# Edge network: transposed destination one-hots by a compare of two tensors

## The reference

```python
def _L1_gnn_ref(x, edge_index, edge_feat, W1, b1, W2, b2, W3, b3):
    source = edge_index[0]
    target = edge_index[1]
    edge = jnp.concatenate([x[source], x[target], edge_feat], axis=-1)   # 48 + 48 + 16
    h = jax.nn.relu(edge @ W1 + b1)                                      # hidden 128
    h = jax.nn.relu(h @ W2 + b2)
    message = h @ W3 + b3
    msum = jax.ops.segment_sum(message, target, num_segments=n)
    cnt = jax.ops.segment_sum(ones, target, num_segments=n)
    return x + msum / jnp.maximum(cnt, 1.0)[:, None]
```

## Time and profile before

| what | us |
|---|---|
| median of 3 runs | 8639.95 (8632.92 to 8644.36) |
| profiled execution, its span | 8640.6 |
| edge network: first gather to last gather | 5516.3 to 7547.1 |
| POOL busy with gathers (1568) | 1554.2 |
| DVE busy with L1849 (392) | 266.8 |
| PE waiting at L1930 for a gather | 263.4 |

### The profile page before, as it was taken

How to read it: one execution, slowest core, us unless ns; L and a number is a source line. 1 busy time by engine, 2 the same in 40 slices (tenths; PEclk the granted TensorE clock), 3 DMA queues, 4 the chain that set the end, 5 groups by cost and what they waited for, 6 DMA issues and landing times. The chain is left out here.

```text
span 8640.6 us, 563982 instructions
## 1 busy us (share of the span) xinstructions
PE 7490.3 (87%) x228719; PEld 6386.0 (74%) x228719; DVE 6536.9 (76%) x13039; ACT 4071.0 (47%) x9117; POOL 5548.3 (64%) x5894
## 2 busy tenths in 40 slices
PE   4967758889999999999999999499999899949794
PEld 4856648889999999999999999344444454449794
DVE  5779979978888898888888888544444444478787
ACT  1229969944444444444444444244444444424242
POOL 2520000068888888888888888477777777738384
PEclk7559975589999999999999999799999999979797
DMA  5210026689999999999999999433333333249495
GB/s 80 92 47 0 0 69 246 247 299 342 338 338 339 340 340 336 340 340 338 340 340 338 339 338 339 122 77 79 78 79 79 79 79 77 64 161 339 161 338 166
DMA packets 833483, 1832.18 MB, mean 212 GB/s; under 512 B 245310, under 2 KB 306774, under 8 KB 831838
## 3 DMA queue, kind: packets, MB, share of 16 engines
q1 hardware_dynamic: 752974, 1777.08, 58.4%
q0 software_dynamic: 59776, 46.03, 4.8%
q10 hardware_dynamic: 20624, 7.81, 0.5%
HBM read 1667.67 MB, written 157.79 MB: 211 GB/s over the span
## 5 line engine op out<-in xcount | busy, mean ns | idle before, releaser
L1491 PE MATMUL banks<-arena 128*128 128x48 bf16 x58800 | 2352.6, 184 | 5.4 <-issue 5.4
L1491 PEld LDWEIGHTS banks<-arena 128*128 128x128 fp8e4 x58800 | 2270.5, 95 | 5.9 <-issue 5.7
L1457 DVE TENSOR_TENSOR banks<-banks,wslot 128x384 f32<-128x384 f32 (+1 forms) x3600 | 1984.5, 569 | 343.8 <-PE banks L1491 309.8
L1391 POOL TENSOR_TENSOR arena<-arena 128x768 bf16<-128x768 f32 (+2 forms) x1200 | 1838.3, 1540 | 422.6 <-DVE arena L1461 414.1
L1323 ACT CAST arena<-banks 128x384 bf16<-128x384 f32 (+1 forms) x2400 | 1178.8, 493 | 1872.6 <-DVE banks L1457 1693.7
L1491 PE MATMUL banks<-xc,arena 128*128 128x48 bf16 x24500 | 1943.0, 184 | 62.0 <-DVEq L1470 14.9
L1491 PEld LDWEIGHTS banks<-xc,arena 128*128 128x128 fp8e4 x24500 | 1864.4, 95 | 164.5 <-issue 104.7
L1773 POOL DMA_INDIRECT f<-node_table,idx x1568 | 1554.2, 991 | 557.6 <-issue 466.9
L1461 DVE TENSOR_TENSOR arena<-banks,arena 128x384 f32<-128x384 f32 (+1 forms) x2400 | 1350.4, 574 | 95.4 <-ACT arena L1323 2.3
L1505 PE MATMUL banks<-arena 32*128 32x144 bf16 x80400 | 1374.8, 222 | 21.5 <-issue 13.3
L1505 PEld LDWEIGHTS banks<-arena 32*128 32x128 bf16 x80400 | 1261.2, 93 | 49.2 <-issue 17.8
(11 more groups left out here) (385 smaller groups left out, 13650.6 us busy)
## 6 DMA issues: line engine op xcount, KB each, us to landing
arena<-onehots SPq DMA_DIRECT2D x1200, 512.0 KB, 4.9
arena<-onehots SPq DMA_DIRECT2D x1500, 256.0 KB, 5.2
arena<-onehots SPq DMA_DIRECT2D x300, 576.0 KB, 5.8
arena<-onehots SPq DMA_DIRECT2D x300, 544.0 KB, 5.3
arena<-in_dst SPq DMA_DIRECT2D x195, 512.0 KB
arena<-onehots SPq DMA_DIRECT2D x300, 288.0 KB
onehots<-arena SPq DMA_DIRECT2D x100, 768.0 KB, 3.2
arena<-key_rows SPq DMA_DIRECT2D x196, 196.0 KB
```

Of the source, the lines that this page charges most:

```text
L1391: nc.gpsimd.tensor_tensor(mp_low[b], mp_rest[b], mp_mid[b], ALU.subtract).then_inc(lo_done[b], 1)
L1457: nc.vector.tensor_tensor(bank, bank, w, ALU.mult).then_inc(m_done, 1)
L1491: m = nc.tensor.matmul(to, g_ring[b][:, i * P:(i + 1) * P], x_part, start=c == 0, stop=c == 2)
```

## The change

The compare of `turn_dst` becomes another form of instruction. Before, VectorE compared one tensor with a scalar per partition, the column g of `row_w`. Now it compares two tensors: the second is the same column, read with a step of zero over all 4 x 128 elements. Place, order, destination, waits and signals stay as they are.

```diff
@@ -1846,8 +1846,8 @@
                         when(dve, dst_in[u], t * 16 + 16)
                         when(dve, transposed, q + (FREE - 1))
                         mine = dst_rows[:, u, :].rearrange("p (e k) -> p k e", k=TILES)[:, HALF * j:HALF * j + HALF, :]
-                        nc.vector.tensor_scalar(hotT[:, j, :].rearrange("p (k e) -> p k e", k=HALF), mine,
-                                                row_w[:, bass.ds(g, 1)], None, ALU.is_equal).then_inc(hotT_ready, 1)
+                        nc.vector.tensor_tensor(hotT[:, j, :].rearrange("p (k e) -> p k e", k=HALF), mine,
+                                                row_w[:, bass.ds(g, 1)].unsqueeze(2).broadcast_to([P, HALF, P]), ALU.is_equal).then_inc(hotT_ready, 1)
```

## The result

The changed kernel takes **8672.5 us** (median of 5 runs, 8669.4 to 8684.2); beside it the kernel before took 8641.1 (5 runs). The ratio is 1.0036, with an interval of 1.0024 to 1.0048: slower by about 31 us. The forecast was 8692, slower, with a range of 8622 to 8755. The profiled execution is 30.0 us longer than the one before.

The account below looks back on a forecast made before the run. GpSimd's gathers were taken to pace the edge stage. 8640.6 + 51 (gathers held longer) + 0 (VectorE's extra work, hidden) = 8692 us; the 8-in-10 range was 8622 to 8755.

Parts of the forecast that it names:

- What bounds the stage: Edge network's stage: GpSimd's gathers pace it one after the other, 1.25 us each, about 10 us a group.
- (a) the instruction's time: L1849: two-tensor form takes 1.07 us instead of 681 ns, priced from L947; ends 678 and 1225 ns.
- (b) VectorE's extra work at nothing: VectorE: 392 x 0.39 = 153 us more work, hidden off the path, put at 0.
- the nearest reader: L1939, taken to load one-hots that end behind L1849, with 0.49 us of room.
- (c) the gathers: Gathers stretched longer by L1849: +86 us for an even spread, +51 us after leaving out tied groups.
- evenly spread: Compares fall at any phase of the gathers' beat; each costs (T - 0.12)^2 / (2 x 1.25) on average.
- late moment: Late point of a gather held by the scalar L1849: 6 of 70 us of stretching, gone after the change.
- The share of tied groups: 80 of 196 groups, where TensorE waits for the gather, counted at no change; 0.59 of 86 us left.
- The 0.12 us: Taken off what is left of a running compare to get what a gather's start loses.
- the two-tensor form holds nothing: Rival: two-tensor L1849 does not hold gathers, all 55 us of its stretching go, 8586 us; 8%.
- The short compare: Rival: L1849 stays at 678 ns, only the late 6 us go, 8635 us; 8%.
- The engines falling into step: Rival: compares settle at a good phase of the gathers' beat, 15 us less than now, 8626 us; 14%.

Follow-up runs that it names:

- dense: Changed kernel's two-tensor compare reading 512 neighbouring row numbers instead of every eighth one: 8606.4 us, ratio 0.9963 to the kernel before.
- the one-tensor compare: Kernel before, its scalar compare given an unused running sum and the low 16 bits of row numbers as input: 8573.8 us, ratio 0.9924.
- the moved order: Changed kernel with the odd half-steps' compare L1849 placed behind the subtraction L1880: 8758.1 us, ratio 1.0133 to the kernel before.

## Why the prediction was right, and where its sizes were off

*What bounds the stage* was right: the table above is the same statement with eleven kernels.

*(a) the instruction's time*: 1.07 forecast, 1.076 measured. L947 was the right neighbour, and the stepping is the reason: dense, it takes 0.685.

*(b) VectorE's extra work at nothing*: right, and shown by the one-tensor compare, which is longer still. But I misread the nearest reader. The one-hots of L1862 that end at 7530.89 are not those that L1939 loads at 7531.38: they are made two half-steps ahead (`L_HOT` 8, `L_SUM` 10), so the room is a whole group's step, not 0.49 us. The reader with little room is L1930, whose weight load waits for L1849. What ended TensorE's idle time at L1930 (us, times), before and after:

```profile
  DVE arena L1849: 119.5, 150
```

```profile
  DVE arena L1849: 112.0, 106
```

So that did not grow either.

*(c) the gathers* is where the size was off: +51 forecast, +30 measured. By its own terms:

| term | forecast | measured |
|---|---|---|
| L1849 at the start, before | 49 | 40.2 |
| L1849 at the start, after | 141.5 evenly spread | 92.0 |
| late moment, freed | 6 | 12.1 |
| L1880 | no change | 10.1 less |

The growth at the start, scaled by 0.59 as I did, is 92.5 x 0.59 = 55, and 51.8 came. The miss is in the other two: the late moment was worth double, and L1880, which I left out of the sum, lost most of what it cost. I had found the 6 by taking two evenly spread terms from the 70, so all that the even spread said too much at the start was missing there; counting the late stretches in the trace of before would have given 12.

*The share of tied groups* came out near the mark, but its reason is half right. With a wait of over 0.3 us at L1930 as the sign of a tied group, there are 79 before and 103 after. They cost 0.54 us of stretching each before and 0.52 after: no change, as I had counted them, though they are not the same groups in the two traces. In the others it rose from 0.235 to 0.49, that is by 0.26 and not by the 0.44 of the even spread, so a phase decides there too. That 55 lies so near to 51.8 is therefore in part luck. And it is not a property of tied groups: in the moved order they cost 0.98 each. I can't say why the phases settle as they do in each kernel; the pairs' distance explains why one of two is paid, and a full account of where a pair begins against the beat stays open.

*The 0.12 us* at the end of a compare is 0.175 under the stepping two-tensor form. With it the even spread gives (1.076 - 0.175) squared / 2.5 x 392 = 127 instead of 141.5.

*The rivals.* That the two-tensor form holds nothing is refuted by 176 of 179 gathers. The Trainium skill, "SBUF — State Buffer", section "Who interferes with whom", has the rule that fits: a VectorE instruction with two inputs in SBUF contends with a GpSimd instruction that reads SBUF. The same section of the Trainium skill reports a probe in which `tensor_tensor` did not stall transfers. For these gathers the runs show otherwise: from 0.94 to 1.67 in the rows above. The short compare is refuted by 1076. The engines falling into step was half true: in 151 of 195 pairs one compare of the two comes out free, and the cost is 92 where the even spread has 127, though not below that of the kernel before.

## What to carry to other kernels

Where GpSimd's gathers pace a stage, sum their busy time first and compare kernels by it; then ask of each vector instruction not only how long it is but whether it reads one tensor or two, whether it works in the two-at-a-time form, and how its distance to the next such instruction stands to the gathers' beat. In these runs a long instruction that holds nothing was better than a short one that does (8574 against 8637), and two short ones were better than one long (8606 against 8673). An even spread of phases bounds such a cost well enough for its sign, but not for its size: the same edit cost 31 us in one order of the code and 101 in another.

## What was not expected of the hardware

A compare with a scalar that also writes a running sum takes 1134 ns and 83 for reading the sum, where the same without it takes 681, and it holds no gather at either moment. A vector instruction that reads one tensor from PSUM and one from SBUF (L1871) holds none either: in the trace after, 113 gathers started with more than 0.25 us of it left, and none was stretched. With the holds gone, TensorE waits for a gather in nearly every group, 193 times, but for a shorter time each (311 us, against 263 in 80 waits before; 97 of either is the first wait, ahead of the loop). Of waits over 2.2 us there are 3 instead of 34. Its granted clock, a mean over the span at 1.2 and at 2.4 GHz, was 0.906 to 0.938 of the higher level in the five runs, and 0.891 to 0.925 in the nine of the kernel before beside them. The two profiled executions, with 0.938 and 0.892, lie near opposite ends of this, so most of what they differ by is no effect of the kernel. A compare with its row numbers in PSUM, which the same theory would let through, was not tried: the loop's tiles take all eight banks.
